# Criss-cross attention on one core: scores and attention of an image interleaved with the next image's projections

## What is computed

```
q = Wq x + bq;  k = Wk x + bk;  v = Wv x + bv           (1x1 convolutions)
eH = q . k along the column of the pixel, own pixel = -inf;  eW = q . k along its row
att = softmax over the 192 values of eH and eW together
out = gamma * (v attH + v attW) + x
```

## Time and profile before

| | us |
|---|---|
| median of 3 runs | 4679.86 |
| lowest, highest | 4664.12, 4681.54 |
| the profiled execution | 4648.17 |
| its span, first to last instruction | 4646.0 |
| TensorE busy (82% of the span) | 3813.5 |
| VectorE busy (66%) | 3080.0 |
| ScalarE busy (40%) | 1860.9 |
| GpSimd busy (15%) | 704.0 |

### The profile page before, as it was taken

One profiled execution on the slowest core, in us unless ns is written; L12 is line 12 of the kernel. 1 busy time (PEld: TensorE's weight loads), 2 busy tenths in 40 slices (PEclk: granted clock), 3 DMA queues, 4 the chain that ended last, 5 costly groups with the idle time before them and its releaser, 6 DMA issues.

```text
span 4646.0 us, 122516 instructions
## 1 busy us (share of the span) xinstructions
PE 3813.5 (82%) x39768; PEld 2805.1 (60%) x39768; DVE 3080.0 (66%) x4371; ACT 1860.9 (40%) x3947; POOL 704.0 (15%) x979
## 2 busy tenths in 40 slices
PE   3997789977899768997789867898778977789777
PEld 1557665566655665566755667555775557745577
DVE  6667566675676756767557676576765767667575
ACT  1554135541355313553145522455314543245431
POOL 0113001130011300113011130111301113011120
PEclk9997789977898878988799787897879978799687
DMA  7765987669876798757977489775897759977599
GB/s 251 236 216 189 297 263 232 204 210 287 258 231 187 227 299 244 231 172 255 294 246 235 147 271 293 240 236 163 265 290 241 233 180 262 289 228 231 176 270 277
DMA packets 1130201, 1109.71 MB, mean 239 GB/s; under 512 B 48528, under 2 KB 979856, under 8 KB 1127824
## 3 DMA queue, kind: packets, MB, share of 16 engines
q1 hardware_dynamic: 1044624, 803.63, 61.2%
q10 hardware_dynamic: 85248, 302.03, 17.9%
HBM read 775.16 MB, written 301.99 MB: 232 GB/s over the span
## 4 chain that ended last, share of the span: by engine, by line
PE 32%; DMA 22%; DVE 13%; issue 13%; ACT 10%; SPq 6%; ACTq 2%; POOL 1%; DVEq 1%; POOLq 0%
DMA v_in<-v_pixel_major 17%; PE banks L1019 10%; PE banks L898 5%; DMA x_raw<-x 4%; PE banks L900 4%; PE banks L899 4%; SPq L389 4%; ACT x_hi L476 3%; PE banks L919 3%; PE banks L916 3%; DVE x_lo L696 3%; DVE acc L874 3%; ACT prob_row L512 2%; DVE nmax L754 2%; DVE xmax_blk L651 2%
## 5 line engine op out<-in xcount | busy, mean ns | idle before, releaser
L860 DVE SCALAR_TENSOR_TENSOR acc<-banks,scales,acc 128x384 f32 x1152 | 862.8, 782 | 540.0 <-PE banks L1019 520.8
L898 PE MATMUL banks<-wv_hi,x_hi 128*128 128x512 f16 x2304 | 881.5, 383 | 231.4 <-DVE x_lo L696 231.4
L1019 PE MATMUL banks<-prob_col,v_in 96*128 96x96 f16 x12288 | 704.1, 225 | 234.1 <-DMA v_in<-v_pixel_major 185.6
L899 PE MATMUL banks<-wv_lo,x_hi 128*128 128x512 f16 x2304 | 880.6, 382 | 0.0
L900 PE MATMUL banks<-wv_hi,x_lo 128*128 128x512 f16 x2304 | 879.7, 382 | 0.0
L1019 PE MATMUL banks<-prob_row,v_in 96*128 96x96 f16 x12288 | 699.1, 224 | 156.9 <-DMA v_in<-v_pixel_major 120.6
L1019 PEld LDWEIGHTS banks<-prob_col,v_in 96*128 96x128 f16 x12288 | 652.9, 109 | 286.5 <-issue 207.0
L570 ACT ACTIVATE acc<-acc,gbv_col (+1 forms) x384 | 358.7, 934 | 1143.1 <-DVE acc L860 1102.0
L1019 PEld LDWEIGHTS banks<-prob_row,v_in 96*128 96x128 f16 x12288 | 650.1, 109 | 199.2 <-issue 98.9
L696 DVE SCALAR_TENSOR_TENSOR x_lo<-x_raw,scales,x_hi 128x1024 f16<-128x1024 f32 x288 | 391.7, 1362 | 548.6 <-ACT x_hi L476 548.6
L427 POOL TENSOR_TENSOR q_low<-qk_f,q_both 64x256 f32 x288 | 191.7, 666 | 3016.3 <-ACT k_hi L495 2992.3
(11 more groups left out here) (90 smaller groups left out, 4405.3 us busy)
## 6 DMA issues: line engine op xcount, KB each, us to landing
v_in<-v_pixel_major SPq DMA_DIRECT2D x768, 384.0 KB, 8.4
x_raw<-x SPq DMA_DIRECT2D x288, 512.0 KB, 4.3
x_next<-x SPq DMA_DIRECT2D x288, 512.0 KB, 3.8
v_pixel_major<-v_out SPq DMA_DIRECT2D x576, 256.0 KB, 2.6
out<-acc ACTq DMA_DIRECT2D x384, 384.0 KB, 5.9
acc<-x ACTq DMA_DIRECT2D x16, 4608.0 KB, 19.0
acc<-x ACTq DMA_DIRECT2D x192, 384.0 KB, 8.9
x_first<-x SPq DMA_DIRECT2D x36, 512.0 KB, 7.5
```

The source lines that it names most:

```text
L860: nc.vector.scalar_tensor_tensor(out=a, in0=out_bank[m % 4], scalar=scales[:, O_FACTOR:O_FACTOR + 1], in1=a, op0=ALU.mult, op1=ALU.add,).t ...
L898: nc.tensor.matmul(dst, s_hi, m_hi, start=(t == 0), stop=False)
L899: nc.tensor.matmul(dst, s_hi, m_lo, start=False, stop=False)
L1019: last = nc.tensor.matmul(dst[:, g, :], v, parts[o][:, h * G + g, c, :], start=(a == 0 and c == 0), stop=(a == 1 and c == 1),)
```

## The change

The unit of projection work becomes an item. Blocks have 384 pixels, so 24 an image, with three v tiles and one q and k block each: 96 items. The first image's 96 items run alone. Then come 7 batches: batch b does scores and attention of image b, and between them, at fixed places in each engine's stream, the items of image b + 1. 8 items stand ahead of the first score pair (HEAD), one before each of the 24 pairs, 5 around the statistics (STATS), and 59 among the 192 attention groups, about 3.25 groups after each item. The last image's batch has no items.

- q and k no longer stay in SBUF. ScalarE casts the whole block (`qk_hi`), GpSimd subtracts once, SP stores both to device memory (`qk`), and at the start of a batch 12 DMAs bring them back in halves (`load_qk`), after all residual adds and output stores of the batch before.
- Attention does three products, not four: low v with low probability is left out.
- One accumulator for a channel tile. The column direction's result is written to it by ScalarE, with scale and bias (`evacuate_column`); VectorE adds the row direction (`add_row`); GpSimd adds x from a ring of six chunks of 768 pixels (`add_residual`) and ScalarE stores that chunk. x for it is loaded by SP (`load_residual`).
- PSUM: two banks for v tiles, one for q and k, two pairs for scores; in the attention three output banks and two for transposes. Rings of 4 for `v_out`, 2 for `e_grp`.
- The scan of the next x reads 24 contiguous pieces of 6144 bytes per partition instead of 36 blocks, in the first items of a batch (`load_next`, `see_next`), two images ahead of the attention.
- The batch is written out; only the loop over batches is a loop.

The core of the diff (empty lines left out):

```diff
--- before.py
+++ after.py
...
+    BLK = 4 * W
     PT = BLK // P
     NB = HW // BLK
-    assert NB % 2 == 0 and HW % BLK == 0
+    assert BLK % P == 0 and NB % 2 == 0 and NB * PT % 4 == 0
+    SUBS = PT + 1
+    ITEMS = NB * SUBS
     G = 4
     NG = L // G
     NP = NG // 2
-    SP = 4
-    NS = NP // SP
-    BODY = 2 * (2 * G * W) // (2 * BLK)
-    NJ = NB // 2 // BODY
-    assert BODY * 2 * BLK == 2 * (2 * G * W) and NJ * BODY * 2 == NB and 2 * NJ == NP
-    U = 4
-    NI = NG // U
-    assert NG % U == 0 and G * L * 4 <= 2048
+    PAIRS = 2 * NP
+    GROUPS = CT * 2 * NG
     VS = 2 * G
     VU = 6
-    NV = L // VS // VU
-    assert L % (VS * VU) == 0
-    PH3 = CT * 2 * NV * VU
+    NL = L // VS
+    LOADS = CT * 2 * NL
+    assert LOADS % VU == 0
+    XR = 6
+    NCH = L // VS
+    CHUNKS = CT * NCH
+    CPX = VS * W
+    assert CHUNKS % XR == 0
+    SCAN = HW * CT // (4 * BLK)
+    NXT = 4
+    LAG = 2
+    AHEAD = 2
+    NE = 2
+    OUTS = 3
+    V_OUT = 4
+    HEAD = 8
+    STATS = 5
+    S_ITEMS = HEAD + PAIRS + STATS
+    T_ITEMS = ITEMS - S_ITEMS
...
+            def load_qk(b):
+                for s in range(2):
+                    wait_alone(sp, qk_stored[s], (b + 1) * (ROUNDS["x"] * 32) + 32)
+                wait_alone(sp, res_added, b * CHUNKS + ONE0)
+                halves = [slice(c * HW // 2, (c + 1) * HW // 2) for c in range(2)]
+                for c, px in enumerate(halves):
+                    sp.dma_start(q_both[0:CQ, px], qk[b, 0, 0:CQ, px]).then_inc(qk_loaded[c], 16)
+                    sp.dma_start(q_both[CQ:P, px], qk[b, 1, 0:CQ, px]).then_inc(qk_loaded[c], 16)
+                    sp.dma_start(k_hi[0:CQ, px], qk[b, 0, CQ:P, px]).then_inc(qk_loaded[c], 16)
+                    sp.dma_start(k_hi[CQ:P, px], qk[b, 0, CQ:P, px]).then_inc(qk_loaded[c], 16)
+                for u in range(XR):
+                    wait_alone(sp, out_stored[u], b * (ROUNDS["xr"] * 16) + 16)
+                for c, px in enumerate(halves):
+                    sp.dma_start(k_lo[0:CQ, px], qk[b, 1, CQ:P, px]).then_inc(qk_loaded[c], 16)
+                    sp.dma_start(k_lo[CQ:P, px], qk[b, 1, CQ:P, px]).then_inc(qk_loaded[c], 16)
...
+            def load_residual(b, i):
+                t, c = divmod(i, NCH)
+                u = i % XR
+                if i >= XR:
+                    sp.wait_ge(out_stored[u], b * (ROUNDS["xr"] * 16) + (i // XR) * 16 + 16)
+                sp.dma_start(xr[u][:, :], x_acc[b, t, :, c * CPX:(c + 1) * CPX]).then_inc(xr_loaded[u], 16)
+            def batch(b, items):
+                load_qk(b)
+                for k in range(HEAD + PAIRS):
+                    if items:
+                        item(b + 1, k)
+                        if k < SCAN:
+                            if k == 0:
+                                wait_alone(sp, o_mm, b * GROUPS + ONE0)
+                            load_next((b + 2) % B, b + 1, k)
+                if items:
+                    wait_alone(sp, xmax_own_ready, b + 3)
+                for k in range(V_OUT):
+                    wait_alone(sp, v_stored[k], (b + 1) * (ROUNDS["v"] * 16) + 16)
+                wait_alone(sp, o_mm, b * GROUPS + ONE0)
+                for i in range(VU):
+                    load_v(b, i)
+                wait_alone(sp, s_ready, (b + 1) * PAIRS)
+                for i in range(XR):
+                    load_residual(b, i)
+                for k in range(STATS):
+                    if items:
+                        item(b + 1, HEAD + PAIRS + k)
+                for k in range(T_ITEMS if items else GROUPS):
+                    if items:
+                        item(b + 1, S_ITEMS + k)
+                    for g in groups_after(k, items):
+                        if g % 2 and (g - 1) // 2 + VU < LOADS:
+                            load_v(b, (g - 1) // 2 + VU)
+                        late = g - 6
+                        if late >= 0:
+                            t, o, h = group_at(late)
+                            if o == ROW and h % 2 and t * NCH + h // 2 + XR < CHUNKS:
+                                load_residual(b, t * NCH + h // 2 + XR)
...
+            def add_residual(b, i):
+                t, c = divmod(i, NCH)
+                u = i % XR
+                pool.wait_ge(xr_loaded[u], b * (ROUNDS["xr"] * 16) + (i // XR) * 16 + 16)
+                pool.wait_ge(row_added, (b * CT + t) * NG + 2 * c + 2 + ONE0)
+                nc.gpsimd.tensor_tensor(
+                    xr[u][:, :], xr[u][:, :], acc[:, c * CPX:(c + 1) * CPX], ALU.add
+                ).then_inc(res_added, 1)
...
+            def evacuate_column(b, g):
+                t, o, h = group_at(g)
+                if h == 0:
+                    act.wait_ge(res_added, (b * CT + t) * NCH + ONE0)
+                act.wait_ge(o_mm, b * GROUPS + g + 1 + ONE0)
+                nc.scalar.activation(
+                    acc_strips[COL][:, h * G:(h + 1) * G, :], out_bank[g % OUTS], ACT.Identity,
+                    scale=att[:, O_FACTOR:O_FACTOR + 1], bias=gbv_col[:, t:t + 1],
+                ).then_inc(col_evac, 1)
...
+            def batch(b, items):
+                wait_alone(dve, row_added, b * (CT * NG) + ONE0)
+                wait_alone(dve, proj_ready, b + 2)
+                nc.vector.tensor_copy(att[:, :], att_next[:, :]).then_inc(att_ready, 1)
+                dve.wait_ge(att_ready, b + 1)
+                for k in range(HEAD + PAIRS):
+                    if items:
+                        item(b + 1, k)
+                    if k >= HEAD:
+                        score_pair(b, k - HEAD)
+                    if items and LAG <= k < SCAN + LAG:
+                        see_next(b + 1, k - LAG)
+                    if items and k == SCAN + LAG:
+                        see_all(b + 1)
...
+            def item(m, i):
+                n, sub = divmod(i, SUBS)
+                s = n % 2
+                if sub == 0:
+                    pe.wait_ge(x_split, m * NB + n + 1 + SPLIT0)
+                if sub < PT:
+                    tile = n * PT + sub
+                    px = slice(sub * P, (sub + 1) * P)
+                    pe.wait_ge(v_ready, m * (NB * PT) + tile - 2 + V_READY0 + 1)
+                    three_products(
+                        bank[tile % 2][:, :],
+                        lambda t: (x_hi[s][:, t, px], x_lo[s][:, t, px]),
+                        lambda t: (wv_hi[:, t, :], wv_lo[:, t, :]),
+                    ).then_inc(v_mm, 1)
+                else:
+                    pe.wait_ge(qk_evac, m * NB + n + ONE0)
+                    three_products(
+                        bank[2][:, 0:BLK],
+                        lambda t: (wqk_hi[:, t, :], wqk_lo[:, t, :]),
+                        lambda t: (x_hi[s][:, t, :], x_lo[s][:, t, :]),
+                    ).then_inc(qk_mm, 1)
...
+            def score_pair(b, p):
+                o, q = pair_at(p)
+                if p == 0:
+                    pe.wait_ge(row_added, b * (CT * NG) + ONE0)
+                    pe.wait_ge(qk_loaded[0], (b + 1) * 96)
+                if p == NP // 2:
+                    pe.wait_ge(qk_loaded[1], (b + 1) * 96)
+                pe.wait_ge(e_ready, b * PAIRS + p - 2 + E0 + 1)
+                for u in range(2):
+                    dst = strip_bank[4 + 2 * (p % 2) + u]
...
+            def attend(b, i):
+                t, o, h = group_at(i)
+                if i < 2 * NG:
+                    pe.wait_ge(p_ready, b * (2 * NG) + i + 1 + P0)
+                if h % 2 == 0:
+                    load = i // 2
+                    pe.wait_ge(v_loaded[load % VU], b * (ROUNDS["load"] * 16) + (load // VU + 1) * 16)
+                if i >= OUTS:
+                    pt, po, ph = group_at(i - OUTS)
+                    if po == COL:
+                        pe.wait_ge(col_evac, (b * CT + pt) * NG + ph + 1 + ONE0)
+                    else:
+                        pe.wait_ge(row_added, (b * CT + pt) * NG + ph + 1 + ONE0)
+                dst = out_bank[i % OUTS]
...
+                    v_hi, v_lo = v_in[u][:, (h % 2) * G + g, 0, :], v_in[u][:, (h % 2) * G + g, 1, :]
+                    p_hi, p_lo = parts[o][:, h * G + g, 0, :], parts[o][:, h * G + g, 1, :]
+                    nc.tensor.matmul(dst[:, g, :], v_hi, p_hi, start=True, stop=False)
+                    nc.tensor.matmul(dst[:, g, :], v_hi, p_lo, start=False, stop=False)
+                    last = nc.tensor.matmul(dst[:, g, :], v_lo, p_hi, start=False, stop=True)
+                last.then_inc(o_mm, 1)
+            def batch(b, items):
+                for k in range(HEAD + PAIRS):
...
+                for k in range(HEAD + PAIRS):
+                    if items:
+                        item(b + 1, k)
+                    if k >= HEAD:
+                        score_pair(b, k - HEAD)
+                for k in range(STATS):
+                    if items:
...
+                for i in range(AHEAD):
+                    transpose_group(b, i)
+                for k in range(T_ITEMS if items else GROUPS):
```

(9 more changed lines are left out.)

1006 lines of the change are left out of this document (473 added, 533 removed).

## The result

The changed kernel took 4835.9 us (median of 4 runs, 4834.5 to 4836.4), the kernel before 4676.5 us beside it. The ratio is 1.034, with a 95% interval of 1.032 to 1.037: slower by 3.4%, where 4585 us, 2% faster, was forecast.

What follows compares the result with a forecast made beforehand. TensorE was taken to bind projections and DMA the last three attention tiles. Start 62, first projections 245, seven periods of 551 and last image 387 gave 4551, plus 2, times 1.0068: 4585 us, range 4210 to 4960.

Steps and rivals of the forecast that it cites:

- Seam and head: Start of a batch, 8 items without scores waiting behind stores and the query/key reload: 30 us, bounds 22 and 45.
- My own test: Sign of a wrong forecast: TensorE waiting at the seam over 20 us for v_out stores or the reload.
- the first attention tile: Attention of the first channel tile, with transposes added: 43 us column half plus 52 us row half.
- hand-over of the accumulator: Where a tile ends, column evacuation waits for the last residual add: costed at nothing, 6 us a period if uncovered.
- the three tiles: Attention of the other three channel tiles, with projection items beside it: 83.5 us each, 250 us in all.
- better-overlap rival: Small and large packets pass each other in attention: row half 48 us, period 502, 4240 us; chance 0.20.
- ceiling rival: Large transfers in long mixes held to 358 GB/s: row half 56 us, period 569, 4720 us; chance 0.10.
- My split of a tile: Attention tile: row half 52 us, bound by DMA; column half 32 us, with TensorE at full clock.
- a row pair with its item: Score stage, one row-score pair and one projection item: 6.1 us.
- a column pair: Score stage, one column-score pair and one projection item: 6.5 us.
- ScalarE's and VectorE's chain: Score stage, the two engines' orders wait on each other: 4.7 to 7.7 us an item, 6.2 mean.
- clock rival: TensorE's clock falls to 1.2 GHz in the score stage: pairs 178 us, period 598, 4915 us; chance 0.25.

Runs made afterwards that it cites:

- e2: Changed kernel with queries and keys reloaded in 6 transfers of 128 partitions instead of 12 of 64, rows in wrong places: 4715.9 us, ratio 1.012.
- e11: e6 with the reload in six transfers of 128 partitions, rows of q and k in wrong places: 4569.9 us, ratio 0.979.
- e6: e1 with the next image's third x block loaded after the last residual load and its first split made four groups before the end: 4687.7 us, ratio 1.004.
- e1: Changed kernel with GpSimd's cross-partition maximum of the next x moved from the first attention items to the score stage: 4739.0 us, ratio 1.016.
- e16: e6 with q and k stored as channels, high or low, pixels; six 128-partition reloads, rows interleaved, whole computation kept: 4579.0 us, ratio 0.981.
- e14: e6 with the high 64 partitions of q_both and k_hi reloaded from GpSimd's queue beside SP's low ones: 4673.6 us, ratio 1.002.
- e15: e6 with q and k stored as q or k, high or low, 64 rows, reloaded in six 128-partition transfers: 5474.7 us, ratio 1.173.
- e10: e1 with ScalarE's column evacuation written in row order instead of strided, columns added in wrong places: 4715.3 us, ratio 1.010.

## Why the prediction was wrong

- **The first failed step is "Seam and head, 8 items without scores ... I take 30 (bounds 22 and 45)".** It took 72. Of the 42 us too little, the reload's half rate is 14 (e2, and e11 against e6): I priced its 7.1 MB from rows of transfers that fill 128 partitions. The order at the seam is 8 (e6 against e1): I listed what SP does after the seam, and not what stands before it in SP's queue and in ScalarE's program. The other 20 (50 in e16 against 30) stay when both are repaired. There TensorE idles 5.7, 2.5 and 15.8 us, 24 in all, where my 30 left 11: the v stores stand behind a reload that still takes some 17 us (7.1 MB at 410), with four tiles in v_out. The ninth item is 2.6 of the rest, and some 5 are the clock: TensorE's work there, 22 us at full clock, took 26.6 at a mean of 0.77. The mechanism was in the text, the length of the drain and the clock behind it were not. My own test, "TensorE waiting at the seam over 20 us for v_out stores or the reload", came true: 10.2 and 23.6 us for v_out, and 9.7 for the first split.
- **The second is the first attention tile, 95 against 121 (mean of six batches).** The change moves a GpSimd reduction of 0.38 us and I gave it no price, because in the kernel before it is hidden; e1 shows 13 us a period for it. What hid it was idle time of GpSimd in the column scores; in the first tile's column half, TensorE's transposes wait for GpSimd's normalisations. Without it this half takes 42.7 us, for 43 forecast. The other 14 us are in the row half, 66 for 52, and no edit here moved them by more than 2. I had it bound by transfers, but the DMA share is 0.72 there. In e16 GpSimd is busy for 41 of its 67 us and stands 23.6 us before its residual adds, waiting for VectorE's row adds, while normalisations that TensorE needs are queued behind. So GpSimd's order is the suspect; but no run took its adds out of that half, and the cause stays open.
- **Where a tile ends I costed the hand-over of the accumulator at nothing.** It was not covered: TensorE waited 1.7, 6.8 and 4.8 us for it early in the three tiles of the batch above. The stage came out short all the same, because its other parts were priced too high.
- **What held.** Projections beside the transfer-bound attention pay: the three tiles took 80 us each at a DMA share of 1.09, for 83.5 forecast and 78 by the better-overlap rival. The ceiling rival (88 a tile) is out. My split of a tile was wrong: from start to start TensorE takes 36, 39 and 35 us for the row halves and 33, 52 and 46 for the column halves, where 52 and 32 were forecast. It runs through a row half on what lies in the buffers, and part of the residuals' transfers is paid in the column half behind it: those of the last two tiles moved 14.2 and 13.1 MB, their row halves 12.0 and 10.4.
- **Two terms were too large.** From start to start a row pair with its item took 5.4 us, for 6.1, and a column pair 5.6, for 6.5. The 5.6 is the sum of TensorE's two prices in the text, 3.21 and 2.43: in the last of these pairs TensorE is busy all the time, at full clock. ScalarE's and VectorE's chain, which I let bind, did not. The clock was 0.92 in this stage, so the clock rival (178 us at 1.2 GHz) was wrong. It said "slower", and the kernel is slower; that is luck. Statistics are 21 to 23 us, near the 25.
- **The fourth product** was costed as hidden, and it is: 10 us in all.
- "Small errors, multiplied by 7, decide the sign" was the right warning: 36 us a period were enough. The chance of slower, 0.36, hung mostly on the clock; only 0.04 of it was for errors of the forecast's own terms, whose bound for the seam ended at 45.

## What to carry to other kernels

When a step is moved to another stage, price it again by what its engine does in the new stage: a 0.4-us GpSimd operation of another kind cost 13 us a period where other GpSimd work was due. Price a transfer by its partitions and its outermost dimension, not by bytes alone: fill 128 partitions from a pattern whose outer dimension is large (64 and 128 ran at full rate here, 2 left most engines idle), and use the freedom of a sum over partitions to choose the layout. At a seam between two images, list every queue's entries before and after it in order; an old image's last load must not stand behind a new image's first. And a total that comes out right proves no stage: compare stage by stage.

## What the runs showed of the hardware

- Transfers to 64 partitions ran at 220 GB/s (changed kernel, all DMA engines busy), those to 128 at about 410 with rows of the same length (e16); halves issued from two queues together still at 227 (e14).
- An outermost dimension of 2: 49 to 66 GB/s, a DMA share of 0.1 (e15).
- GpSimd: 7.07 us before a reduction over partitions and 7.24 after it, around 0.38 us of work (changed kernel).
- ScalarE writing 384 fp32 values from PSUM with a stride: 996 ns, in order: 670 (e10).
